# Masks of the first attention moved to GpSimd with its values woven into the scores, and 64-row keys in the gated attention

## The reference

```
x = x + attention(norm(x))            # 16 heads of 8, causal, online softmax
x = x + experts(norm(x))              # top 2 of 8
x = x + random_feature_attention(norm(x))
x = x + experts(norm(x))
x = x + gated_attention(norm(x))      # 8 heads of 64, decay per channel
x = x + fp4_ffn(norm(x))
x = x + retention(norm(x))
x = x + fp4_ffn(norm(x))
```

```
# first: per head, d = 8
scores = scale * Q K^T;  scores[key later than query] = -inf
m = max(scores);  p = exp(scores - m);  O = (p V) / sum(p)
# fifth: per head, state S of 64 x 64, a = sigmoid(x Wa + ba), k = k / |k|
S = a * S + k v^T;   o = S^T q
```

## Time and profile before

| | us |
|---|---|
| median of three runs (lowest, highest) | 1256.01 (1245.17, 1256.72) |
| the profiled execution, its own time | 1249.02 |
| its span, first to last instruction | 1247.2 |
| PE busy | 1007.8 |
| DVE busy | 835.9 |
| ACT busy | 387.6 |
| POOL busy | 294.5 |
| mean granted TensorE clock | 0.867 |

### The profile page before, as it was taken

The page is one execution under the profiler, slowest core; times in us unless marked ns, Lnnn a source line. Parts: engine busy times, 40 slices in busy tenths (PEclk is TensorE's granted clock), DMA queues, the critical chain, the costliest instruction groups (busy, mean ns, idle before and its releaser), DMA issues.

```text
span 1247.2 us, 16823 instructions
## 1 busy us (share of the span) xinstructions
PE 1007.8 (81%) x6275; PEld 619.5 (50%) x6275; DVE 835.9 (67%) x2001; ACT 387.6 (31%) x634; POOL 294.5 (24%) x249
## 2 busy tenths in 40 slices
PE   3798988979989897679897862999999566897465
PEld 2254555543434565543333331776768345676344
DVE  5666758756565467767666566648555896688895
ACT  1154445533333243423232254112211222231121
POOL 3600000003222433303222213121110344233232
PEclk8689889989999787779888896899999887787786
DMA  8633030020000000000000000000000000000000
GB/s 239 161 103 78 2 78 2 3 89 1 1 1 0 1 2 1 2 1 0 1 1 0 1 0 3 1 1 1 1 1 2 0 1 1 2 2 2 1 9 25
DMA packets 9948, 25.40 MB, mean 20 GB/s; under 512 B 979, under 2 KB 7315, under 8 KB 9171
## 3 DMA queue, kind: packets, MB, share of 16 engines
q1 hardware_dynamic: 9568, 23.49, 6.6%
q10 hardware_dynamic: 294, 0.79, 0.3%
HBM read 16.73 MB, written 7.34 MB: 19 GB/s over the span
## 4 chain that ended last, share of the span: by engine, by line
PE 54%; DVE 31%; issue 6%; ACT 4%; POOL 3%; DMA 2%; DVEq 0%; SPq 0%; ACTq 0%; POOLq 0%
PE ps L686 5%; DVE a_MN L359 4%; PE ps L673 4%; PE ps L678 4%; PE ps L252 3%; PE ps L194 2%; DVE XN L117 2%; PE ps L1507 2%; PE ps L1568 2%; PE ps L1522 2%; PE ps L1565 2%; PE ps L2098 2%; PE ps L214 2%; PE ps L1940 2%; POOL rs L96 1%
## 5 line engine op out<-in xcount | busy, mean ns | idle before, releaser
L359 DVE TENSOR_REDUCE a_MN<-ps 128x1 f32<-128x384 f32 (+3 forms) x176 | 107.4, 639 | 59.6 <-PE ps L197 57.5
L96 POOL TENSOR_TENSOR rs<-t,mhalf 128x4 f32<-128x4 f32 x37 | 37.4, 1011 | 382.8 <-DVE t L90 382.5
L930 POOL TENSOR_TENSOR f_Y<-f_Y,f_TT 128x512 f32<-128x512 f32 x56 | 70.8, 1265 | 179.4 <-DVE f_TT L820 179.4
L465 ACT ACTIVATE a_PT<-ps 128x1024 f32<-128x1024 f32 x64 | 65.1, 1024 | 69.9 <-PE ps L218 68.9
L895 ACT ACTIVATE f_HH<-ps,pack_zero 128x512 f32<-128x512 f32 x64 | 44.0, 687 | 132.9 <-PE ps L673 132.9
L143 DVE TENSOR_TENSOR X<-ps,X 128x512 f32<-128x512 f32 x32 | 22.0, 687 | 92.7 <-PE ps L1578 49.4
L194 PE MATMUL ps<-a_KS,a_QS 72*128 72x128 bf16 (+3 forms) x256 | 70.5, 337 | 14.1 <-DVE a_MN L359 10.9
L686 PE MATMUL ps<-f_HH,pack_zero 128*128 128x512 f32 x128 | 73.9, 660 | 5.7 <-DVE f_TT L820 5.7
L811 DVE TENSOR_TENSOR f_XS<-ps,XNT 128x512 f32<-128x512 f32 x64 | 43.9, 688 | 49.2 <-PE ps L666 49.2
L673 PE MATMUL ps<-f_XS,pack_zero 128*128 128x512 f32 x128 | 69.9, 630 | 1.3 <-DVE f_XS L811 1.3
L820 DVE SCALAR_TENSOR_TENSOR f_TT<-ps,pack_zero,f_X 128x512 f32<-128x512 f32 x64 | 47.9, 749 | 32.5 <-PE ps L686 32.5
(11 more groups left out here) (310 smaller groups left out, 2322.4 us busy)
## 6 DMA issues: line engine op xcount, KB each, us to landing
scratch<-a_parts SPq DMA_DIRECT2D x16, 384.0 KB, 4.3
a_QS<-scratch SPq DMA_DIRECT2D x3, 1152.0 KB
a_KS<-scratch SPq DMA_DIRECT2D x9, 384.0 KB
pack_one<-in_one SPq DMA_DIRECT2D x1, 2679.5 KB, 9.3
pack_zero<-in_zero SPq DMA_DIRECT2D x1, 2653.5 KB, 16.3
a_QS<-scratch SPq DMA_DIRECT2D x4, 288.0 KB
a_KS<-scratch SPq DMA_DIRECT2D x12, 96.0 KB
X<-in_x SPq DMA_DIRECT2D x4, 256.0 KB, 10.1
```

The costliest lines, as they stand in the source:

```text
L96: pool.tensor_tensor(M.rs[:, 4 * b:4 * b + 4], M.t1[:, 4 * b:4 * b + 4], M.mhalf[:, 0:4], ALU.pow).then_inc(root.sem, root.tick(n, b))
L359: dve.tensor_reduce(M.a_MN[:, n % 2, ti, h0:h0 + k], bank(M, M.bank["a_max", n, jj], 128 * (ti + 1) * k).rearrange("p (a c) -> p a c", a=k ...
L465: act.activation(M.a_PT[:, c % 6, 0:1024], M.ps[:, a * 512:a * 512 + 1024], ACT.Exp).then_inc(made.sem, made.tick(n, hh))
L930: pool.tensor_tensor(M.f_Y[:, i, :], M.f_Y[:, i, :], M.f_TT[:, u % 3, :], ALU.add).then_inc(made.sem, made.tick(n, u))
```

## The change

In the first attention the masks `late` leave the score matmuls. POOL's new `seen` sets the elements of `a_PT` below the diagonal to zero after the exponential, with `affine_select` in place. `values` is cut in four calls, one by key block, and each is placed among the scores and maxima of the next group; it waits for `a_seen`. `a_PT` has eight buffers; `turned`, `evict` and `normalize` move one group later; `back`, `output`, the residual and the norm of a batch move by one group. `a_OT` and `a_ON` now lie in the memory of `a_f`.

In the gated attention `h_KZ` is unpadded: the two heads' keys lie in rows 0 to 63 and 64 to 127, each score matmul takes 64 rows, and the two heads alternate in two banks. The keys are turned by four transposes of 128 columns. DVE makes the keys with four products instead of eight. The key lengths are computed by quarters between the query projections, ACT's exponentials of the next batch come between the copies of the turned keys, and the memsets of `h_KZ` on POOL go. The random-feature attention is the same in both kernels.

```diff
-        late(bank(M, a, 128).unsqueeze(1))
         scores(b, h, 1, bank(M, a + 1, 384))
-        scores(b, h, 3, bank(M, a + 1, 128, 384), False)
-        late(bank(M, a + 1).rearrange("p (a c) -> p a c", a=4)[:, 0:4:3, :]).then_inc(scored.sem, scored.tick(n, hh))
+        scores(b, h, 3, bank(M, a + 1, 128, 384)).then_inc(scored.sem, scored.tick(n, hh))
...
+    def values(n, si):
+        if si == 0:
+            take(pe, M, 5)
+            if g == 0:
+                pe.wait_ge(S["a_va"].sem, S["a_va"].at(b))
+            pe.wait_ge(S["a_seen"].sem, S["a_seen"].at(n, "tail", 1))
+        for j in range(4):
+            m = pe.matmul(bank(M, 5, N, 128 * si, 32 * j, 32 * j + 32), M.a_VA[:, i, si, 4 * g + j, :],
+                          M.a_PT[:, (4 * n + j) % 8, A_AT[si]:A_AT[si] + N],
+                          start=(si == 0), stop=(si == 3), skip_group_check=True)
...
+        b, g, ahead = n // 4, n % 4, range(11) if n + 2 < 16 else range(0)
+        for hh in range(4):
+            for jj in ahead[3 * hh:3 * hh + 1]:
+                maxima(n + 2, jj)
+            exps(n, hh)
+            for jj in ahead[3 * hh + 1:3 * hh + 2]:
+                maxima(n + 2, jj)
+            if hh % 2:
+                tail(n, hh // 2)
+            if hh == 1 and n + 1 < 16:
+                rows(n + 1)
+            if n:
+                values(n - 1, hh)
+            for jj in ahead[3 * hh + 2:3 * hh + 3]:
+                maxima(n + 2, jj)
+            if hh == 0 and g == 1 and b + 1 < 4:
+                plain(b + 1)
+            if hh == 0 and g == 2 and b:
+                back(b - 1)
+            if hh == 1 and n >= 2:
+                turned(n - 2)
+            if hh == 2 and g == 2 and b:
+                output(b - 1)
...
+    def seen(n, half):
+        made, c = S["a_seen"], 4 * n + 2 * half
+        for u in range(2):
+            P = M.a_PT[:, (c + u) % 8, 0:1024].rearrange("p (a t) -> p a t", a=2)[:, :, 0:128]
+            pool.wait_ge(S["a_exped"].sem, S["a_exped"].at(n, 2 * half + u))
+            pool.affine_select(P, P, [[0, 2], [1, 128]], ALU.is_ge, 0.0, base=0, channel_multiplier=-1).then_inc(made.sem, made.tick(n, 2 * half + u))
+        P = M.a_PT[:, c % 8:c % 8 + 2, 896:1152].rearrange("p h (a t) -> p h a t", a=2)
+        pool.wait_ge(S["a_exped"].sem, S["a_exped"].at(n, "tail", half))
+        pool.affine_select(P, P, [[0, 2], [0, 2], [1, 128]], ALU.is_ge, 0.0, base=0, channel_multiplier=-1).then_inc(made.sem, made.tick(n, "tail", half))
...
+            pe.matmul(bank(M, bk), M.g_wq[:, 128 * c:128 * c + 128], M.XNT[:, tok], start=True, stop=True).then_inc(q.sem, q.tick(b, c))
             M.freed[bk] = (S["h_qz"], (b, c))
+            lengths(b, c)
...
+            for c in range(4):
+                for r in range(2):
+                    row = slice(64 * r, 64 * r + 64)
+                    m = pe.matmul(bank(M, pair[r], 128, 128 * c), M.h_KZ[row, c, tk], M.h_QZ[row, i, c, tk], start=True, stop=True, skip_group_check=True)
...
                 for c in range(4):
-                    for q in range(2):
-                        m = pe.matmul(bank(M, bk, 64, 128 * c + 64 * q), M.h_KZ[:, q, c, tk], M.ident[:, 64 * q:64 * q + 64], start=True, stop=True)
+                    m = pe.transpose(bank(M, bk, 128, 128 * c), M.h_KZ[:, c, tk], M.ident[:, :])
...
-            for r in range(2):
-                row = slice(64 * r, 64 * r + 64)
-                dve.tensor_tensor(M.h_KZ[row, r, c, :], bank(M, bk)[row, :], M.h_EK[row, c, :], ALU.mult).then_inc(kz.sem, kz.tick(b, c))
+            dve.tensor_tensor(M.h_KZ[:, c, :], bank(M, bk), M.h_EK[:, c, :], ALU.mult).then_inc(kz.sem, kz.tick(b, c))
...
             act.activation(M.h_KT[:, j, :], bank(M, M.bank["h_kt", b, j]), ACT.Copy).then_inc(made.sem, made.tick(b, j))
+            if b + 1 < 4:
+                factors(b + 1, j)
```

More of the change, by code:

```diff
@@ L210, in rows, with scores @@
         M.freed[bk] = (S["a_mt"], (n,))
-    def scores(b, h, si, out, first=True):
+    def scores(b, h, si, out):
         i = b % 2
[L214 to L219, removed]
+        return pe.matmul(out, M.a_KS[0:75, i, h, 128 * si:128 * si + 128], M.a_QS[0:75, i, h, 128 * si:512], start=True, stop=True)
     def exps(n, hh):
@@ L237, in tail @@
         take(pe, M, 4)
-        for u in range(2):
-            scores(b, h + u, 2, bank(M, 4, 256, 256 * u), u == 0)
-        late(bank(M, 4).rearrange("p (a c) -> p a c", a=2)[:, :, 0:128]).then_inc(scored.sem, scored.tick(n, "tail", half))
+        scores(b, h, 2, bank(M, 4, 256))
+        scores(b, h + 1, 2, bank(M, 4, 256, 256)).then_inc(scored.sem, scored.tick(n, "tail", half))
         M.freed[4] = (S["a_exped"], (n, "tail", half))
[L243 to L256, removed]
+    def values(n, si):
+        b, g, i, valued, N = n // 4, n % 4, n // 4 % 2, S["a_valued"], 512 - 128 * si
+        if si == 0:
[7 more added lines that the diff above has]
+                          start=(si == 0), stop=(si == 3), skip_group_check=True)
+        if si == 3:
+            m.then_inc(valued.sem, valued.tick(n))
+            M.freed[5] = (S["a_ol"], (n,))
     def turned(n):
@@ L301, in attn_a_tensor @@
     for n in range(16):
[L302 to L328, removed]
-                tail(n, 1)
-                if more:
-                    maxima(n + 2, 10)
-                if g == 1 and b:
-                    output(b - 1)
-    values(15)
+        b, g, ahead = n // 4, n % 4, range(11) if n + 2 < 16 else range(0)
[21 more added lines that the diff above has]
+                output(b - 1)
+            if hh == 3 and g == 3 and b:
+                turn_tensor(pe, S, M, 1, b - 1, side(M), M.XN, (S["normed"], (1, b - 1)))
+    turned(14)
+    for si in range(4):
+        values(15, si)
     turned(15)
@@ L536, in attn_a_gpsimd @@
         split(b, "k")
-    for b in range(4):
-        norm_root(pool, S, M, 1, b)
+    for n in range(16):
+        b, g = n // 4, n % 4
+        for half in range(2):
+            seen(n, half)
+        if g == 2 and b:
+            norm_root(pool, S, M, 1, b - 1)
+    norm_root(pool, S, M, 1, 3)
 def spread_rows(sp, b, name, scr, dst, done, event, heads=slice(0, 16)):
@@ L1508, in project, with lengths @@
             M.freed[bk] = (S["h_qz"], (b, c))
+            lengths(b, c)
+    def lengths(b, j):
+        n2 = S["h_n2"]
+        if j == 0:
+            take(pe, M, 7)
+        for c in range(4):
+            if j == 0:
+                pe.wait_ge(S["h_sq"].sem, S["h_sq"].at(b, c))
+            m = pe.matmul(bank(M, 7, 2, 8 * j + 2 * c), M.h_SQ[:, c, 128 * j:128 * j + 128], M.sel_64[:, :], start=True, stop=True)
+        if j == 3:
+            m.then_inc(n2.sem, n2.tick(b))
+            M.freed[7] = (S["h_clip"], (b,))
     def scores(b):
-        i = b % 2
+        i, scored, turned, value = b % 2, S["h_scored"], S["h_kturn"], S["h_v"]
         pe.wait_ge(S["h_kz"].sem, S["h_kz"].at(b, 3))
@@ L1514, in scores @@
         if b == 0:
[L1515 to L1533 removed]
+            pe.wait_ge(S["h_zero"].sem, S["h_zero"].at(0))
```

157 lines of the change are left out of this document (76 added, 81 removed).

## The result

The changed kernel takes 1268.98 us (median of four runs, 1266.54 to 1273.96) where the kernel before took 1250.85 (1245.17 to 1256.72): a ratio of 1.015, with a 95% interval of 1.008 to 1.022. It is slower, by 18 us, where the forecast was 1237 and the range ended at 1262. The profiled execution took 1266.54 us with a span of 1264.8; against the profiled 1249.02 that is +17.5.

What follows compares the result with a forecast made beforehand. The first attention was taken as bound by nothing alone, the gated attention by PE. 1249.0 - 5.5 (first attention) - 13.3 (gated attention) = 1230.2 us profiled, 1237 against the median; range 1216 to 1262.

Steps and rivals of the forecast that it cites:

- the sum of the gated stage: Gated attention: shorter PE work, limited by DVE, was to save 13.3 us over the four batches.
- the rival that had it: Gated scores: PE's idle time drops the clock, each batch gives its gain back, total 1249 us; chance 0.28.
- a new PE wait for DVE's key product before the second query: Gated attention, sign of being right: PE reaches its second query matmul about 3 us before DVE frees a bank.
- DVE's walk: Gated attention, steady batch: DVE limits the gain; scores phase shortens by 0.6 us, output starts 1.5 us sooner.
- The first gated batch: Gated attention, first batch: 2 us from its projection, 3.8 from the scores, 2.5 from the next projection.
- PE's count of 30 us: Gated attention: key turns, scores and key lengths were to take 7.6 us a batch off PE, 30 in all.
- The pairs of scores on 64 rows: Gated scores: eight paired matmuls take 1.3 us, including 0.3 for changing tiling; 1.9 us saved a batch.
- PE stays the bound: Rival: DVE has more slack and selects are fast; -28 us gated, -10 first attention, total 1218; chance 0.17.
- The select: First attention, POOL: 1.05 us for 512 elements, 0.6 for 256, giving an iteration of 10.7 us instead of 11.2.
- Each stays between work that DVE and PE do anyway: First attention: `back`, `output`, residual and norms move one iteration later, taken to add no time.
- The end: End of the first attention: costs 1.5 us more, with nothing to cover the last select and group 14's transposes.
- The slow select: Rival, first attention: 3 us for 512 elements makes each iteration 13.4 us, total 1272; chance 0.13.

Runs made afterwards that it cites:

- experiment 4: The changed kernel with six unread 512-column matmuls a batch added on PE in the gated attention, from the second batch on: 1246.85 us, ratio 0.9957.
- experiment 8: The kernel before with six unread 512-column matmuls a batch added in the gated attention: 1265.21 us, ratio 1.0079.
- experiment 6: The changed kernel with DVE's factors, norm and rounding in the gated attention moved behind the next batch's keys: 1223.39 us, ratio 0.9738.
- experiment 12: The changed kernel with the gated attention's DVE work moved and the key turns made by eight 64-column matmuls again: 1243.85 us, ratio 0.9908.
- experiment 5: The changed kernel with the gated key turns made by eight 64-column matmuls again instead of four transposes: 1270.46 us, ratio 1.0117.
- experiment 9: The kernel before with only DVE's factors, norm and rounding moved out of the gated attention's scores phase: 1252.59 us, ratio 0.9988.
- experiment 10: The changed kernel with both DVE moves, the gated attention's work and the first attention's norm ahead of later reductions: 1221.48 us, ratio 0.9742.
- experiment 1: The changed first attention with the gated attention as in the kernel before: 1251.87 us, ratio 0.9995.
- experiment 3: The changed kernel with the first attention's second norm half moved from before normalize to between the second and third reduction: 1263.34 us, ratio 1.0101.
- experiment 7: The changed kernel with three unread matmuls a batch added in the gated attention, after the second pair of scores: 1269.41 us, ratio 1.0132.

## Why the prediction was wrong

**The step that failed: the sum of the gated stage put the clock at nothing, and the rival that had it, at 0.28, priced it too low.** The term was -13.3 and measured +12.0; with the clock held at 1.00 in the batches (experiment 4) the stage took 8.0 less than before, so the clock is some 20 of the 25 us that were missed. The rival gave the fall 3 us a batch: "the 6 us of states and key projection behind the scores". Measured it was 4.1 and 14.3 us on two batches against the kernel before, and 4.8 and 15.0 against the same kernel with its clock held (experiment 4). The price was too low since it took the fall to end with the phase behind the wait. In the trace of the second batch the states and keys ran at 1.00 (853 to 860), and the lower level lay over scores, queries and the head of the output; in the third it reached over the queries and nearly the whole output (916.96 to 947 at 0.50), solid PE work. Half clock in the score phases, which the prediction named as a sign of being wrong, is there too. That the chance was too low is argued and not shown: the rival was tied to one place. The forecast itself contained a second, "a new PE wait for DVE's key product before the second query", expected at about 3 us, with its cost in time but not in clock. It came, with 1.76 us for the 3 (863.44), and the window around it, 862 to 880, has 0.72. A forecast that lets PE wait at two places a batch should have priced all the work behind both. Experiment 4, with experiment 8 as its control, shows that the clock was the cause: 22 us came back with more work. The rival's end was wrong too: it stood within 1% of the kernel before, and no case of the prediction ended slower by this mechanism.

**DVE's walk held, up to the queries.** The first state sum came at 854.92, 13.0 us after the factor step ended (841.90), where before it took 13.5: 0.5 sooner, forecast 0.6. The key product began 0.99 sooner, of which 0.47 is the batch's own earlier start. From the query that waits for the key product to the output "5 us" were forecast and 8.5 came (863.44 to 871.94, part of it at half clock), so the output started at 871.94 rather than 1.5 before 870.01. So the term of 1.5 a steady batch failed first through this stretch, not through the scores. At full clock the walk gave 0.7 a steady batch (46.86 for 47.56), half of the 1.5; the six fillers are in that number and may hold part of it.

**The first gated batch** gave 4.7 of the 8.3 forecast. Its head is at a low clock in both kernels, and for how long differed by some 11 us between profiled executions (experiments 6 and 12), so this term can't be read closer. In the profile of experiment 5, where the clock is up from 784 on, the same stretch took 102.79, 12.0 less than before, even with the old turns.

**PE's count of 30 us was right in sum but not due**: 29 from experiment 9 to 6, 3.3 a batch for the turns (3.2 forecast). The pairs of scores on 64 rows ran to the next start in 1.10 us, forecast 1.3 with 0.3 of it for the changes of tiling. The Trainium skill (TensorEngine Tiling (Array Packing), Key Properties) has the drain at such a change; here little of the 0.3 was seen between scores and turns. The rival "PE stays the bound", 1218, was nearly met by experiments 6 and 10 in the gated stage, which is what it said would happen if DVE had more slack; of its 10 us in the first attention nothing came, though the selects were fast.

**First attention: sum -5.5, measured +1.1 in the profile, within 0.3% of nothing in experiment 1.** Three terms:
- *The select* was taken at 1.05 us and took 0.64, near the cast's 0.61 that was the lower bound. The group went to 10.08 us; by the prediction's own rule, 0.1 us a group for each 0.1 of the select, it would be 10.3. This term was too cautious and would have made the error larger. The Trainium skill (GPSIMD Engine Reference, section 3.1) leads to 0.77 for a one-input loop of this size; the measurement is 0.64, and decides.
- *"Each stays between work that DVE and PE do anyway"*, of the norm and its neighbours, was wrong. The norm's 1.9 us stood in front of `normalize`, PE waited 1.68 us, and the clock fell: two groups of 16.3 and 16.2 in place of 11.75, +9 us. The place in the queue explains only a part: with the norm ahead of the reductions the groups still took 15.2 and 15.3, and the first attention gained 3.3 in the profile (experiment 3). What makes up the rest of the 9 isn't separated.
- *The end* cost more: the last short group 8.8 us for 6.4, and 17.5 for 15.4 from there to the sum, 4.5 against 1.5.

The two groups whose end a transfer sets gave nothing together, as said: from first score matmul to first score matmul 16.29 us for 15.28, and 14.56 for 15.59. The slow select and pairs that don't overlap are both refuted.

**What stays open**: why the clock falls at one wait and not at a like one. In experiment 7 the two long batches changed places, in experiment 5 two executions of ten escaped, and in the profile of one of them two waits of 1.76 us were followed by 1.00 and by 0.57. A single profile shows one of these histories, and the runs here don't say which waits may be left.

## What to carry to other kernels

Where an engine is the bound and busy nearly all the time, making its work shorter can create waits, and here waits of PE of 1 to 3 us cost more than the work that was saved: before such a change, move the other engine's work so that it is ready (experiment 6), and do the two together, since here either alone gained nothing. If a faster PE leaves PE slower, look at the granted clock by window first, and test the suspicion with matmuls that nobody reads; if it is wrong they add their own time (12 us in experiment 8), if it is right the kernel gets faster (22 us in experiment 4). A step that is moved in a queue to a place between other work needs the name of what stands behind it there.

## What the runs showed of the hardware

- Waits of PE of 1.3 to 2.8 us, in a stage otherwise full, were accompanied by a clock of 0.5 over stretches as long as 30 us of gapless work (916.96 to 947). Not each wait was: behind one of 1.76 us it stayed at 1.00 (experiment 5, 857.89). By the Trainium skill (TensorE: Matmul & The Clock Gate, "A second HAM failure mode: psum-queue depth-cycling") frequent short idles between groups of matmuls made the clock swing between its levels in a bf16 kernel; the swings of this stage between 1.00 and 0.50 agree. Matmuls without use made the kernel 22 us faster (experiment 4).
- The same program ran on two levels 20 us apart (experiment 5: two executions at 1247 and 1254, eight at 1266 to 1274).
- `affine_select` in place on POOL takes 0.41 us for 128x256 and 0.64 us for 128x512 in fp32.
- Sixteen records of eight fp32 score matmuls from 64 rows, in alternating row halves and banks, pass in 1.10 us (836.91 to 838.01, kernel after); four transposes of 128x128 in fp32 in 0.6 (838.01 to 838.59), where eight 64-column matmuls took 1.73.
